# Attention kernel, two layers: row maxima over pairs of PSUM banks in the global stage, three single score banks, and twelve tiles of maxima moved from one stage to the next

## What is computed

```python
def reference(x, ...):
    x = x + L0(gn(x))
    x = x + L1(gn(x))

def L0(x):
    rel_h = einsum('bhwc,hkc->bhwk', r_q, Rh)
    rel_w = einsum('bhwc,wkc->bhwk', r_q, Rw)
    scores = q @ swapaxes(k, -1, -2) * SCALE + (rel_h + rel_w)
    return (softmax(scores) @ v) @ w_proj.T + b_proj

def L1(x):
    scores = where(neighbourhood_7x7 | register_key, q @ k_cat * scale, -1e30)
    return (softmax(scores) @ v_cat) @ out_w.T + out_b
```

## Time and profile before

| | |
|---|---|
| runs | 4855.43, 4869.68, 4874.59 us, median 4869.68 |
| profiled execution, its own time | 4862.39 us |
| its span, first to last instruction | 4860.6 us |
| PE, DVE, ACT busy | 91%, 63%, 53% of the span |
| granted TensorE clock, mean | 0.967 of full speed |
| one image in the loop | 292.5 us: main1 77.3, out 1 and prep 1 29.7, main0 157.2, out 0 and prep 0 28.3 |

### The profile page before, as it was taken

One profiled execution on the slowest core, in us unless ns is written; L12 is line 12 of the kernel. 1 busy time (PEld: TensorE's weight loads), 2 busy tenths in 40 slices (PEclk: granted clock), 3 DMA queues, 4 the chain that ended last, 5 costly groups with the idle time before them and its releaser, 6 DMA issues.

```text
span 4860.6 us, 97545 instructions
## 1 busy us (share of the span) xinstructions
PE 4446.6 (91%) x32598; PEld 2268.6 (47%) x32598; DVE 3079.8 (63%) x5558; ACT 2594.1 (53%) x3955; POOL 892.4 (18%) x1901
## 2 busy tenths in 40 slices
PE   4879999999999999999999999999999999999988
PEld 3334453544535454453544535454453544535434
DVE  3736667666675756657566675756757566675644
ACT  1533556555564655555555565555546555565564
POOL 4122021222202222021222202222031221202111
PEclk7988999999999999999999999999999999999999
DMA  6333152442514433153442424433253432424402
GB/s 123 87 73 77 44 119 64 100 87 56 107 42 107 88 89 75 44 115 68 100 80 58 101 52 103 91 83 75 45 114 75 100 80 49 103 60 100 88 15 40
DMA packets 235869, 386.05 MB, mean 79 GB/s; under 512 B 58396, under 2 KB 133728, under 8 KB 235360
## 3 DMA queue, kind: packets, MB, share of 16 engines
q1 hardware_dynamic: 189280, 266.13, 23.7%
q10 hardware_dynamic: 21504, 75.51, 7.8%
q0 software_dynamic: 24576, 37.80, 4.9%
HBM read 227.79 MB, written 88.08 MB: 65 GB/s over the span
## 4 chain that ended last, share of the span: by engine, by line
PE 71%; DVE 11%; issue 6%; DMA 5%; SPq 5%; ACT 2%; DVEq 0%; ACTq 0%; POOL 0%
PE P L1143 14%; PE P L1161 13%; PE P L1102 12%; DVE mx L909 7%; PE P L966 5%; PE P L967 5%; PE P L1193 4%; PE P L1214 4%; DMA queries<-oraw 4%; PE P L1110 3%; PE P L1079 3%; SPq L514 3%; DVE mxc L915 2%; PE P L1186 1%; PE P L1231 1%
## 5 line engine op out<-in xcount | busy, mean ns | idle before, releaser
L909 DVE TENSOR_REDUCE mx<-P 128x1 f32<-128x512 f32 x3072 | 1921.3, 684 | 457.4 <-PE P L1102 453.3
L779 ACT ACTIVATE probs<-P 128x1024 f32<-128x1024 f32 x1536 | 1507.5, 1022 | 854.0 <-PE P L1161 853.8
L1102 PE MATMUL P<-K,AR 96*128 96x256 f16 x6144 | 1074.1, 278 | 56.6 <-DMA AR<-biases 29.5
L1161 PE MATMUL P<-AR,K 113*128 113x512 f16 x3072 | 924.9, 383 | 13.2 <-DMA AR<-mrow 12.6
L915 DVE TENSOR_REDUCE mxc<-P 128x1 f32<-128x336 f32 (+1 forms) x1536 | 656.3, 474 | 317.9 <-PE P L1111 315.0
L1143 PE MATMUL P<-probs,V 128*17 128x512 f32 x6144 | 813.5, 601 | 5.7 <-ACT probs L779 5.7
L1102 PEld LDWEIGHTS P<-K,AR 96*128 96x128 f16 x6144 | 532.2, 98 | 581.4 <-DVE mx L909 202.0
L795 ACT ACTIVATE probs<-P 128x320 f32<-128x320 f32 (+3 forms) x1632 | 612.1, 437 | 338.2 <-PE P L1214 268.4
L1161 PEld LDWEIGHTS P<-AR,K 113*128 113x128 f16 x3072 | 213.3, 98 | 670.3 <-ACT probs L779 519.6
L1110 PE MATMUL P<-K,A 112*128 112x320 f16 (+1 forms) x1536 | 405.2, 300 | 68.7 <-DVE mx L909 54.9
L1214 PE MATMUL P<-A,K 113*128 113x320 f16 (+2 forms) x1536 | 428.3, 300 | 14.7 <-ACT probs L795 14.3
(11 more groups left out here) (125 smaller groups left out, 3718.4 us busy)
## 6 DMA issues: line engine op xcount, KB each, us to landing
AR<-biases SPq DMA_DIRECT2D x384, 256.0 KB, 7.9
AR<-queries ACTq DMA_DIRECT2D x96, 512.0 KB, 5.9
biases<-xn SPq DMA_DIRECT2D x128, 256.0 KB, 2.6
AR<-queries ACTq DMA_DIRECT2D x96, 256.0 KB, 8.8
K<-oraw POOLq DMA_DIRECT2D x384, 64.0 KB, 4.7
xin<-in_x_dram SPq DMA_DIRECT2D x16, 768.0 KB, 10.5
queries<-oraw SPq DMA_DIRECT2D x384, 32.0 KB, 4.6
QA<-queries SPq DMA_DIRECT2D x192, 64.0 KB, 2.8
```

What stands on the lines that cost most here:

```text
L779: nc.scalar.activation(probs[:, u % RING, j:j + 2, :], P[:, b:b + 2, :], ACT.Exp).then_inc(p_done[0], 1)
L909: V_.reduce_max(mx[:, n // 2, n % 2:n % 2 + 1], bank, AX.X).then_inc(used, 1)
L1102: last = mm(bank[:, QD * (v % 2):QD * (v % 2) + QD], AR[0:ROWS_MAX[0], part % SLOTS, v, c, j, 128 * q:128 * q + 128], K0[0:ROWS_MAX[0], h, ...
L1161: last = mm(P[:, j, :], K0[0:ROWS, h, 128 * kt:128 * kt + 128], AR[0:ROWS, p % SLOTS, kt // 2, :, j, :], start=True, stop=True)
```

## The change

It does five things.

1. In main0 a `max` job becomes `max2`: two tiles into two neighbouring banks, one DVE reduction over both. In layer 0 the two banks are two halves of one row, so a reduction over 1024 columns gives the final value and the combining reduction goes; in layer 1 one reduction over a view with two rows gives two columns (tiles of equal width are paired, `TILE_PAIRS`).
2. Main0's scores use three single banks 0 to 2: each head's score waits for the exp three scores earlier, and ACT takes exp of 512 columns at a time. The values move to bank 7, and jobs have the four banks 3 to 6.
3. `plan` hands out banks by a ring: a pair starts at an even place and takes two banks, a single job takes one, and a job waits for the latest job that held one of its banks.
4. In main0 the lists follow each other: layer 0 phases 1 (rest) and 2 over steps 0 to 18, `rel` at steps 18, 21, 24 and 27 with layer 1 group 0 over 18 to 30, phases 3, 4, 5 over 29 to 75, layer 1 groups 1 and 2 over 75 to 95.
5. Of phase 1's 32 tiles the last twelve (`SECOND` = 20) and its final move from main1 (and from the jobs ahead of the loop, for image 1) into main0. Main1 keeps single tiles in three banks, and spreads its 20 + 32 layer 0 tiles over the same steps.

```diff
-SCORES, JOBS = (4, 3), 3
-JOB_BANKS = ((4, 5, 7), (3, 4, 5))
+SCORES = 3
+JOB_BANKS, VALUES_BANK = ((3, 4, 5, 6), (3, 4, 5)), 7
...
-def plan(steps, placed):
+def plan(steps, placed, ring):
...
-        before = jobs[len(jobs) - JOBS] if len(jobs) >= JOBS else None
-        after[place].append((len(jobs), job, before))
+        wide = 1 + (job[0] == "max2" and job[4] < ITEMS[job[1]])
+        at += at % wide
+        taken = [ring[(at + k) % len(ring)] for k in range(wide)]
+        before = max((held[b] for b in taken if b in held), default=None)
+        after[place].append((taken[0], job, None if before is None else jobs[before]))
...
-        placed = evenly(max_jobs(0, image, 2), 0, 20)
-    placed += evenly(max_jobs(0, image, 3), 27, 45) + evenly(max_jobs(0, image, 4), 45, 61)
-    placed += evenly(max_jobs(0, image, 5), 61, 77)
-    placed += [(8 + 3 * n, job) for n, job in enumerate(rel_jobs(image, 2))]
+        placed = evenly(max_pairs(0, image, 1)[SECOND // 2:] + max_pairs(0, image, 2), 0, 18)
+    for p in (3, 4, 5):
+        placed += evenly(max_pairs(0, image, p), 15 * p - 16, 15 * p)
+    placed += [(18 + 3 * n, job) for n, job in enumerate(rel_jobs(image, 2))]
...
-        placed += evenly(max_jobs(1, i1, 0), 13, 32)
-        placed += evenly(max_jobs(1, i1, 1) + max_jobs(1, i1, 2)[:THIRD], 73, 95)
+        placed += evenly(max_pairs(1, i1, 0), 18, 30)
+        placed += evenly(max_pairs(1, i1, 1) + max_pairs(1, i1, 2)[:THIRD // 2], 75, 95)
...
-    placed += evenly(max_jobs(0, n0, 0) + max_jobs(0, n0, 1), 25, STEPS[1] - TAIL)
+    placed += evenly(max_jobs(0, n0, 0) + max_jobs(0, n0, 1)[:SECOND], 25, STEPS[1] - TAIL)
...
-                        act.wait_ge(st_done[0], im * STEPS[0] + step + 1)
-                        b = 2 * (step % 2)
-                        nc.scalar.activation(probs[:, u % RING, j:j + 2, :], P[:, b:b + 2, :],
-                                             ACT.Exp).then_inc(p_done[0], 1)
+                        for k in range(2):
+                            single = 2 * step + k
+                            act.wait_ge(st_done[0], im * SINGLES + single + 1)
+                            nc.scalar.activation(probs[:, u % RING, j + k, :], P[:, single % SCORES, :],
+                                                 ACT.Exp).then_inc(p_done[0], 1)
...
+                        elif what == "max2" and layer == 0:
+                            V_.reduce_max(mxc[0][:, n // 2:n // 2 + 1], banks(at, 2), AX.X).then_inc(used, 2)
+                        elif what == "max2":
+                            (a, b), h = TILE_PAIRS[n % TT // 2], n // TT
+                            lo, hi = key_rows(a)
+                            V_.tensor_reduce(mxc[1][:, TT * h + a:TT * h + b + 1:b - a],
+                                             P[:, at:at + 2, 0:W * (hi - lo) + REG], AX.X, ALU.max).then_inc(used, 2)
...
-                        if step >= 2:
-                            pe.wait_ge(p_done[0], im * STEPS[0] + step - 1)
...
-                            last = mm(P[:, j, :], K0[0:ROWS, h, 128 * kt:128 * kt + 128],
-                                      AR[0:ROWS, p % SLOTS, kt // 2, :, j, :], start=True, stop=True)
-                        last.then_inc(st_done[0], 1)
+                            h, single = GH * (p // 2) + j, 4 * u + j
+                            if single >= SCORES:
+                                pe.wait_ge(p_done[0], im * SINGLES + single - SCORES + 1)
...
+                            mm(P[:, single % SCORES, :], K0[0:ROWS, h, 128 * kt:128 * kt + 128],
+                               AR[0:ROWS, p % SLOTS, kt // 2, :, j, :], start=True, stop=True).then_inc(st_done[0], 1)
```

More of the change, by code:

```diff
@@ L78, in max_jobs, with max_pairs @@
     return [("max", layer, image, part, n) for n in range(ITEMS[layer] + 1)]
+def max_pairs(layer, image, part):
+    return [("max2", layer, image, part, n) for n in range(0, ITEMS[layer] + 1, 2)]
 def rel_jobs(image, g):
@@ L104, in cost @@
 def cost(job):
-    return {"rel": 4, "stat": 1, "max": (7, 5)[job[1]]}[job[0]]
+    return {"rel": 4, "stat": 1, "max": (7, 5)[job[1]], "max2": (12, 9)[job[1]]}[job[0]]
 def evenly(jobs, first, end):
@@ L115, in evenly @@
     return placed
-def plan(steps, placed):
-    after, jobs = [[] for _ in range(steps)], []
+def plan(steps, placed, ring):
+    after, jobs, held, at = [[] for _ in range(steps)], [], {}, 0
     for place, job in sorted(placed, key=lambda p: p[0]):
@@ L124, in plan @@
             continue
[L125 to L126 removed]
+        wide = 1 + (job[0] == "max2" and job[4] < ITEMS[job[1]])
[3 more added lines that the diff above has]
+        after[place].append((taken[0], job, None if before is None else jobs[before]))
+        for b in taken:
+            held[b] = len(jobs)
         jobs.append(job)
+        at += wide
     return after
 def in_turn(*jobs):
[L133 removed]
+    return plan(len(jobs), list(enumerate(jobs)), JOB_BANKS[0])
 def last_job(after):
@@ L389, in consumed @@
                 return stat_used[layer], image * 2 + n + 1
-            return smax_used[layer], image * PER_ITEMS[layer] + part * (ITEMS[layer] + 1) + n + 1
+            done = n + 1 + (kind == "max2" and n < ITEMS[layer])
+            return smax_used[layer], image * PER_ITEMS[layer] + part * (ITEMS[layer] + 1) + done
         def rel_view(bank, n, operand):
@@ L529, in moves @@
                     biases_away(image, part)
-                if what == "max" and n == ITEMS[layer]:
+                if what in ("max", "max2") and n == ITEMS[layer]:
                     sp.wait_ge(*consumed(job))
@@ L1046, in banks_read, with run_job @@
                     unread_qkv.clear()
-            def run_job(bank, job, before):
+            def run_job(at, job, before):
                 what, layer, image, part, n = job
+                bank = P[:, at, :]
                 if before:
@@ L1090, in run_job @@
                     pe.wait_ge(k_in[1][part], (image + 1) * PER_K)
+                tiles = [n + k for k in range(2 if what == "max2" else 1)]
                 if n == ITEMS[layer]:
-                    if layer == 0:
-                        pe.wait_ge(comb_done, image * PHASES[0] + part + 1)
+                    if layer == 0 and what == "max2":
+                        pe.wait_ge(*consumed(job[:4] + (n - 2,)))
+                        last = nc.tensor.transpose(bank[0:ITEMS[0] // 2, 0:128], mxc[0][:], ident[:])
+                    elif layer == 0:
+                        pe.wait_ge(comb_done, part + 1 if is_image(image, 0) else image * 2 + part)
@@ L1114, in run_jobs @@
+                last.then_inc(smax_done[layer], 1 if n == ITEMS[layer] else len(tiles))
             def run_jobs(entries, L):
```

80 lines of the change are left out of this document (43 added, 37 removed).

## The result

The changed kernel takes 4904.3 us (median of six runs, 4888.5 to 4914.0), the kernel before 4866.2 (six runs). The ratio is 1.0078, with a 95% interval of 1.0055 to 1.01: **0.8% slower**. Predicted were 4857 and no change. The profiled execution's span is 4898.1, 37.5 longer than before.

A forecast was written before the change was run, and what follows sets the result against it. PE, busy 91%, was taken as the bound. Main0 4.5 more 15 times, main1 4.7 less 14 times and jobs 7.7 less once sum to -6 from 4862.4: 4856, put at 4857 us for the median; range 4765 to 4930.

The forecast's parts named there:

- The pair's reduction: DVE in main0: one reduction over 1024 columns takes 1.22 us, with 1.37 kept for the range.
- the plain unit: Main0 unit with one pair per step: no bank is waited for, 2.81 us, 0.11 less than before.
- the third pair: Main0 units with three pairs: the third finds the first's banks held until 2.36 instead of 1.72, losing 0.64 us.
- main1: Main1 with fewer layer 0 tiles and one final gone, DVE the bound there: 4.7 us less per image.
- the jobs: Jobs ahead of the loop lose twelve tiles and a final: 7.7 us less, once.
- the exps in halves and the increments: Main0: both cost zero; the rival that increments cost up to 10 ns each gave 4872 us, chance 0.04.
- The third score bank: Main0's fourth score: zero cost in plain units; rival, one bank too few, 0.15 us a unit, 4970 us, chance 0.19.
- The rival of the late wait at unit 15: Main0: PE waits at unit 15 for the table after the later `rel`; 2 us late gives 4887 us, chance 0.04.
- the term of main0's waits: PE's waits in main0: 18.5 us against 16.7 before, so main0 161.7, 4.5 us more, 2.7 of it moved work.
- The walk: Stepping through main0's 48 units with the prices and new order to find PE's waits, trusted to some 2%.
- image 0 at zero: Image 0's main0, without layer 1 pairs and with unchanged tile count: zero change, within 2 us.
- the likeliest case: Whole kernel: the forecast's own case, two stages trading time, 4857 us, range 4820 to 4900, chance 0.49.

The follow-up runs named there:

- e5: Kernel before with halved exps, one increment a score and three score banks in main0, one bank unused; ratio to the kernel before 1.0114.
- e12: Changed kernel with image 0's second-phase pairs in steps 0 to 10 instead of 0 to 13; image 0's main0 159.6 us in place of 165.9.
- e2: Changed kernel without the twelve-tile move: second phase's maxima stay in main1 and the jobs ahead of the loop; ratio to the kernel before 1.0042.
- e8: Changed kernel with the layer 1 maxima beside `rel` in main0 as single tiles, all else in pairs; ratio to the kernel before 1.0066.
- e4: Kernel before with one 512-column exp and one increment per score in main0, four score banks kept; ratio to the kernel before 1.0050.
- clean lists: Kernel before with three score banks, four single job banks, late finals and main0 lists not overlapping except early `rel`; 4677.2 us, ratio 0.9624.

## Why the prediction was wrong

**Right.** The pair's reduction (1.22 predicted, 1.220), the plain unit (2.81; 2.83 in the trace), the third pair (0.64 lost; 0.68 in the trace), main1 (4.7 less; 5.3), the jobs (7.7; 8.7), and in main0 the exps in halves and the increments (zero; 0.3). The third score bank is right for plain units, into which its rival put 0.15 and which show none of it; in short units and image 0 it has a price that the prediction left out (e5). The rival of the late wait at unit 15 does not show: units 15 to 37 are 3.0 shorter.

**Wrong, the term of main0's waits.** The walk gave 18.5 of waits and 161.7 in all, 4.5 more than before; main0 takes 165.2 on the mean, 7.2 more than the mean before (158.0; the image of 157.2, from which the walk starts, ran at full clock). The 2.7 that are missing, 15 times, are 41 us, which alone is more than the 24 that part no change from slower. From the image shown, counting time by which one matmul starts later behind the one before than in a plain unit, the waits are some 21.9 and PE's work is 143.9 (143.2 predicted). They lie where the walk had them: 13.9 up to unit 14 (11.7 predicted), 5.0 in 15 to 37 (4.0), 3.0 behind (2.8). 1.7 of the first is no wait but the lower clock behind the stalls around `rel`, which the walk did not have at all; on the mean of images 1 to 15 it is 2.1, and 0.9 before. So places and prices were right in the main, the lower clock was put at nothing, and the sum of many small ones was 2% low. The forecast is a small difference of two such sums, and the 2% of the whole main0, 3.2 us and 15 times that, should have been in the range of the likeliest case; only the early units' share was.

**Wrong, image 0 at zero.** Its main0 is 13.5 longer, of which 6.5 is the wait for the row (e12: 6.3 won back); the rest was not taken apart. The prediction looked at the four small DMAs of the moved final in the loop, where they had room, and not at image 0, where the new list ends the second phase a step later, nearer to the broadcast.

Together 41 and 13.5, less 8 for main1, 1 for the jobs and 2 at the two ends, are the 43.5 between the -6 of the prediction's sum and the 37.5 measured.

**What the parts do.** The halved exps came with 0.5%, in a stage that they do not touch and for a reason that stays open. Giving up a score bank costs 0.6%, and as a fourth job bank it is worth 2.4%. The pairs spend it: 1.4% in the old lists, 1.0 to 1.5% in the new ones, 2.0% in the best ones. The order costs 0.3 to 0.7%, the move 0.4% with pairs in the new lists, at the edge of what the intervals can tell, and nothing that they can tell in the others. In every one of these lists DVE has less to do with pairs, and in none does it help.

## What to carry to other kernels

A buffer that is handed out in larger pieces comes free later, and a piece waits for its last part: here, where PE waits for banks, one more bank in single pieces was worth more than fewer, longer instructions on the engine that empties them. Before work is moved or merged, look at the waits that a short instruction causes behind a long one: moving the finals behind a product that covers their wait gave 1.3%. When a forecast is a difference of two large sums, give it the error of the sums.

## What the runs showed of the hardware

- One reduction over two PSUM banks (1024 columns) takes 1.220 us on DVE, two over one bank each 1.37: the saving of 0.15 a pair is smaller than the 0.68 that PE loses once where it waits for the pair.
- Four row DMAs of 4 KB land in 1.8 to 2.6 us by themselves, and the slowest of them in 6.1 to 8.1 where 768 KB of broadcasts from another queue are issued ahead of the last one or within 0.2 of it (image 0 of e12, and of e2, e8 and the change).
- Behind stalls around `rel` in main0 (PE busy 8.0 of 11.0 us from 1641.5 on, then 5.9 of 6.0 from 1653.0 on), the change's granted clock fell to 1.2 GHz for part of a stretch of 5.6 us (0.70 on the mean); in e4's main1, behind the wait for the queries, for most of 10 us (0.51). With clean lists a main0 lost 0.2 us to it, with the change 2.4.
- With an increment for each 512 columns in place of one for each 1024, and the exps in halves, main0 grew by 0.3 us, some 3 ns for each of the 96 more increments (e4).
